# Cross-attention and gated feed-forward on one core: attention scores in quarters of the array, stacking transfers over all partitions

## The reference, cut to what matters

```python
q = (layernorm(x) @ Wq.T + bq); k = ctx @ Wk.T + bk; v = ctx @ Wv.T + bv     # split in 16 heads of 8
attn = softmax(q @ k.T / sqrt(8)) @ v;  x = x + attn @ Wo.T + bo
h = layernorm(x)
score_out, score_in = softmax(bottleneck_so(h)), softmax(bottleneck_si(h))   # batch norm over all rows, gelu
out  = keep_top32(score_out) * (h @ W) + (h * keep_top32(score_in)) @ W + bias
x = x + out
```

## Time and profile before

| | us |
|---|---|
| median of 3 runs | 564.16 |
| lowest, highest | 558.95, 564.75 |
| the profiled execution | 563.33 |
| its span | 560.8 |

### The profile page before, as it was taken

One profiled execution on the slowest core, in us unless ns is written; L12 is line 12 of the kernel. 1 busy time (PEld: TensorE's weight loads), 2 busy tenths in 40 slices (PEclk: granted clock), 3 DMA queues, 4 the chain that ended last, 5 costly groups with the idle time before them and its releaser, 6 DMA issues.

```text
span 560.8 us, 15570 instructions
## 1 busy us (share of the span) xinstructions
PE 405.9 (72%) x5186; PEld 316.1 (56%) x5186; DVE 440.5 (79%) x2165; ACT 375.1 (67%) x1060; POOL 330.2 (59%) x402
## 2 busy tenths in 40 slices
PE   3467988999998999988992766666666666666432
PEld 1135766777777777777860545545555555445331
DVE  7745666777877777776541799999999999999990
ACT  2425676877788777766655967777677666676652
POOL 6466676887677777562112046666666666666666
PEclk9857999999999999999795555555555555555555
DMA  4888786888887887675000000000000000000000
GB/s 135 177 206 207 193 199 151 194 185 185 192 195 191 206 187 185 161 168 123 4 4 1 0 2 19 19 20 20 19 20 19 20 20 19 20 20 19 19 20 19
DMA packets 138680, 52.78 MB, mean 94 GB/s; under 512 B 105115, under 2 KB 130908, under 8 KB 137052
## 3 DMA queue, kind: packets, MB, share of 16 engines
q1 hardware_dynamic: 136424, 51.27, 37.8%
q10 hardware_dynamic: 2176, 0.52, 0.4%
HBM read 34.47 MB, written 16.78 MB: 91 GB/s over the span
## 4 chain that ended last, share of the span: by engine, by line
DVE 41%; SPq 33%; DMA 9%; PE 7%; issue 5%; POOL 2%; ACT 2%; POOLq 0%; ACTq 0%; DVEq 0%
SPq L273 30%; DVE kst L868 22%; DVE top_next L859 12%; DMA k_scratch<-k_parts 6%; DVE top_first L859 4%; DMA qst<-q_scratch 3%; SPq L258 3%; PE ps_pv L329 1%; PE ps_col L314 1%; POOL kst L963 1%; ACT x2n L550 1%; PE ps_mix L534 1%; PE ps_row L358 1%; PE ps_row L503 1%; SPq L220 1%
## 5 line engine op out<-in xcount | busy, mean ns | idle before, releaser
L738 DVE TENSOR_REDUCE m<-ps_row 128x8 f32<-128x512 f32 x128 | 82.4, 686 | 54.5 <-PE ps_row L358 54.2
L868 DVE MATCH_REPLACE8 kst<-top_next,kst 128x128 f32<-128x128 f32 x384 | 101.2, 282 | 0.0
L545 ACT ACTIVATE pT<-ps_col 128x512 f32<-128x512 f32 x128 | 68.7, 589 | 37.1 <-PE ps_col L314 37.1
L859 DVE MAX8 top_next<-kst 128x8 f32<-128x128 f32 x384 | 78.2, 282 | 0.0
L329 PE MATMUL ps_pv<-vx,pT 128*64 128x18 f32 x2048 | 72.5, 213 | 0.0
L329 PEld LDWEIGHTS ps_pv<-vx,pT 128*64 128x64 f32 x2048 | 66.1, 139 | 6.3 <-issue 4.2
L519 PE MATMUL ps_proj<-wf_sb,x2T 128*128 128x128 f32 x128 | 33.2, 441 | 45.8 <-ACT x2T L682 45.8
L519 PEld LDWEIGHTS ps_proj<-wf_sb,x2T 128*128 128x128 f32 x128 | 28.5, 328 | 52.2 <-ACT x2T L682 52.2
L550 ACT ACTIVATE x2n<-xr,nm,rs 128x128 f32<-128x128 f32 x128 | 52.6, 493 | 4.2 <-POOL nm L888 4.2
L959 POOL TENSOR_SCALAR neg_max<-top_first 128x4 f32<-128x4 f32 x32 | 7.1, 222 | 74.8 <-DVE top_first L859 74.8
L358 PE MATMUL ps_row<-kst,qst 96*64 96x128 bf16 x1024 | 42.3, 226 | 12.1 <-DMA qst<-q_scratch 12.0
(11 more groups left out here) (103 smaller groups left out, 1092.7 us busy)
## 6 DMA issues: line engine op xcount, KB each, us to landing
k_scratch<-k_parts SPq DMA_DIRECT2D x32, 192.0 KB, 3.1
q_scratch<-q_parts SPq DMA_DIRECT2D x32, 192.0 KB, 3.0
kst<-k_scratch SPq DMA_DIRECT2D x32, 192.0 KB
qst<-q_scratch SPq DMA_DIRECT2D x32, 192.0 KB
xr<-in_x_dram SPq DMA_DIRECT2D x16, 256.0 KB, 4.3
cT<-in_ctxT_dram SPq DMA_DIRECT2D x16, 256.0 KB, 3.7
kst<-k_scratch SPq DMA_DIRECT2D x32, 128.0 KB
qst<-q_scratch SPq DMA_DIRECT2D x32, 128.0 KB
```

What stands on the lines that cost most here:

```text
L545: act.activation(pT[:, b % PT_RING, :, :], ps_col[b % 2][:, :, :], ACT.Exp, scale=SCALE).then_inc(act_exp, 1)
L738: dve.tensor_reduce(m32[:, b // 4, :, 4 * j:4 * j + 4].rearrange("q a h -> q h a"), ps_row[b % 2][:, :, :, :], AX.X, ALU.max).then_inc(dve ...
L859: ins = dve.max(top[:, n, :], src)
L868: ins = dve.match_replace(picked[s][:, p, cols], top[:, n, :], src, PICKED)
```

## The change

- Scores: `qst` and `kst` become the two halves of one tensor `stacks`, `kst` with a row of 8 KB like `qst`. Batch `a` has rows 64a to 64a+63 of the contraction. Every row or column matmul is now 64 rows by 64 columns with 64 moving columns, one for each pair and batch, issued in turn over the four quarters of the array: 128 and 128 a group in place of 64 and 64.
- Stacking: three pairs of transfers, each with both batches and two parts, so that 32 rows four partitions apart go out in one DMA; one more DMA sets the four maxima rows of `qst` to zero first. 7 a group in place of 12. Both scratch writes must have landed before any of them. The wait for `act_mT` ahead of them goes; the maxima DMA (on ScalarE's queue in both kernels, as the diff shows) waits for `moved` instead.
- Order: in each quarter of an iteration TensorE does `key_side` and `query_side` back to back, VectorE's steps are ordered anew, `values` pairs its operands by batch, the queries' split on GpSimd waits for the first maxima.
- Start: weights are loaded on ScalarE's queue, VectorE splits the first keys, and part of the first and last layer norm's small steps go to VectorE.
- Where the stages meet: the gelu table is loaded before the last gates, most of the batch norm's constants are worked out on VectorE, and the two repeated norms move behind the first gelu.
- Tail: the last group's final sums go to VectorE, gate by gate and in halves.

```diff
-RUNS = (3, 2, 1)
-STRIDE = 4
-MROWS = 2 * ROWS
-KROWS = MROWS + 4
+MID, HIGH, LOW = 0, 1, 2
+RUNS = ((MID, MID), (HIGH, MID), (MID, HIGH))
+MAX_ROWS = slice(3, 128, 32)
-STACK = 16 * 2 * len(RUNS)
+STACK = 16 * (2 * len(RUNS) + 1)
...
-        qst = [sb(f"qst{s}", [128, HEADS, HALF], BF16) for s in range(STACKS)]
-        kst = [sb(f"kst{s}", [128, HEADS, PAIRS, 2, SEQ], BF16) for s in range(STACKS)]
+        stacks = [sb(f"stacks{s}", [128, 2, HEADS, HALF], BF16) for s in range(STACKS)]
+        qst = [stacks[s][:, 0, :, :] for s in range(STACKS)]
+        kst = [stacks[s][:, 1, :, :] for s in range(STACKS)]
...
+        scratch = [nc.dram_tensor(f"scratch{s}", (2, 2 * PARTS, 128, HALF), BF16).ap() for s in range(2)]
...
+            def two_parts(g, first):
+                return scratch[g % 2][:, first:first + 2].rearrange("a n (i h) t -> a (n i) (h t)", h=HEADS)
+            def stack(g):
+                s, d = g % 2, slot(g)
...
+                wait(sp, k_out[s], WRITES * (g // 2 + 1))
+                wait(sp, q_out[s], WRITES * (g // 2 + 1))
+                wait(sp, pe_col, 8 * (g - STACKS + 1))
+                sp.dma_start(qst[d][MAX_ROWS, :, :].rearrange("r h t -> r (h t)"), fixed_rows[4:8]).then_inc(moved[d], 16)
+                for run, (q_first, k_first) in enumerate(RUNS):
+                    rows = slice(run, 128, 4)
+                    sp.dma_start(kst[d][rows, :, :].rearrange("r h t -> r (h t)"),
+                                 two_parts(g, PARTS + k_first)).then_inc(moved[d], 16)
+                    sp.dma_start(qst[d][rows, :, :].rearrange("r h t -> r (h t)"),
+                                 two_parts(g, q_first)).then_inc(moved[d], 16)
...
                 if there(t + 1):
-                    wait(sp, act_mT, 2 * t)
-                    wait(sp, pe_col, 8 * (t - 1))
-                    stack(t + 1, k_scratch, k_out, k_moved, True)
-                    stack(t + 1, q_scratch, q_out, q_moved, False)
+                    stack(t + 1)
...
+                for hh in range(HEADS // 2):
+                    h = j * (HEADS // 2) + hh
+                    for pp, a in ((0, 0), (1, 1), (1, 0), (0, 1)):
+                        rows = slice(a * 64, a * 64 + 64)
+                        cols = slice((2 * hp + pp) * SEQ, (2 * hp + pp + 1) * SEQ)
+                        mm = pe.matmul(ps_row[a][pp * SEQ:(pp + 1) * SEQ, hh, :], qst[s][rows, h, cols], kst[s][rows, h, cols],
+                                       start=True, stop=True)
...
-                wait(act, pe_col, 8 * (g - STACKS + 1))
+                wait(act, moved[slot(g)], STACK * uses(g))
                 wait(act, act_mT, 2 * g + hp + 1)
-                act.dma_start(qst[slot(g)][MROWS:KROWS, :, hp * 128:(hp + 1) * 128],
-                              mT[:, hp, :]).then_inc(m_moved[hp][slot(g)], 16)
+                act.dma_start(qst[slot(g)][MAX_ROWS, :, hp * 128:(hp + 1) * 128], mT[:, hp, :]).then_inc(m_moved[hp][slot(g)], 16)
...
-            again(0)
-            again(1)
-            act.wait_ge(dve_half, 2)
             act.activation(nothing[:, 1:2], nothing[:, 0:1], ACT.Gelu)
```

More of the change, by code:

```diff
@@ L236, in _, with write_parts @@
             sp.dma_start(gates[2 * GATES:2 * GATES + 1, :], ones_row).then_inc(rest_in, 16)
[L237 to L247, removed]
+            def write_parts(g, parts, first, done):
                 s = g % 2
                 if parts is k_parts:
-                    wait(sp, gp_split, 4 * g + 4)
+                    wait(sp, dve_ksplit, 4)
+                    wait(sp, gp_split, 4 * g)
                 else:
@@ L262, in stack @@
+            def stack(g):
                 s, d = g % 2, slot(g)
[L263 to L273, removed]
+                if g < STACKS:
+                    wait(sp, gp_zero if g == 1 else dve_zero, 1 + g // 2)
+                    sp.dma_start(kst[d][MAX_ROWS, :, :].rearrange("r h t -> r (h t)"), fixed_rows[0:4]).then_inc(rows_in[d], 16)
+                wait(sp, k_out[s], WRITES * (g // 2 + 1))
[8 more added lines that the diff above has]
+                                 two_parts(g, q_first)).then_inc(moved[d], 16)
@@ L305, in key_side @@
                     wait(pe, m_moved[hp][s], 16 * uses(g))
[L306 to L316, removed]
+                wait(pe, act_exp, 8 * g + 4 * hp + 2 * j)
+                for hh in range(HEADS // 2):
[3 more added lines that the diff above has]
+                        cols = slice((2 * hp + pp) * SEQ, (2 * hp + pp + 1) * SEQ)
+                        mm = pe.matmul(ps_col[a][pp * SEQ:(pp + 1) * SEQ, hh, :], kst[s][rows, h, cols], qst[s][rows, h, cols],
+                                       start=True, stop=True)
+                        if hh == HEADS // 2 - 1 and pp != a:
+                            mm.then_inc(pe_col, 1)
             def values(g, hp, j):
@@ L346, in out_proj, with query_side @@
                 mm.then_inc(pe_out, 1)
[L348 to L360, removed]
+            def query_side(g, hp, j):
+                s = slot(g)
+                if hp == 0 and j == 0:
+                    wait(pe, moved[s], STACK * uses(g))
+                    if g < STACKS:
+                        pe.wait_ge(rows_in[s], 16)
+                wait(pe, dve_max, 8 * g + 4 * hp + 2 * j)
+                for hh in range(HEADS // 2):
+                    h = j * (HEADS // 2) + hh
+                    for pp, a in ((0, 0), (1, 1), (1, 0), (0, 1)):
+                        rows = slice(a * 64, a * 64 + 64)
+                        cols = slice((2 * hp + pp) * SEQ, (2 * hp + pp + 1) * SEQ)
+                        mm = pe.matmul(ps_row[a][pp * SEQ:(pp + 1) * SEQ, hh, :], qst[s][rows, h, cols], kst[s][rows, h, cols],
+                                       start=True, stop=True)
+                        if hh == HEADS // 2 - 1 and pp != a:
+                            mm.then_inc(pe_row, 1)
             def turn_max(g, hp):
@@ L431, in _ @@
                     key_side(t - 1, 0, 0)
+                if c:
+                    query_side(t, 0, 0)
                 if e:
@@ L644, in _ @@
                     wait(act, gp_rs2, 4 * (t - 2) + 4)
+                    wait(act, dve_nm2, 1 if t - 2 == GROUPS - 1 else 0)
                     wait(act, pe_x2T, t - 3)
@@ L696, in _ @@
                             ins.then_inc(a2_exp, 1)
-                if there(t - 1):
+                if there(t - 1) and t < GROUPS:
                     s = (t - 1) % 2
@@ L854, in _ @@
                         else:
-                            wait(dve, d2_rep, 8 * g + 2 * rnd - 1 + half)
-                        for n in range(4 * half, 4 * half + 4):
+                            wait(dve, d2_rep, 8 * g + 2 * rnd - 1 + (1 if by_gate else half))
+                        for n in sets[half]:
                             p, cols = chain(n)
```

372 lines of the change are left out of this document (223 added, 149 removed).

## The result

| | before, us | after, us |
|---|---|---|
| median (4 runs each) | 563.23 | 883.25 |
| lowest, highest | 558.95, 564.75 | 882.87, 884.4 |
| span of the profiled execution | 560.8 | 881.1 |
| mean granted TensorE clock | 0.737 | 0.643 |

The changed kernel takes 1.574 times as long, 95% interval 1.566 to 1.581. The forecast was 917 us, within 855 to 1,020.

What follows compares the result with a forecast made beforehand. Stage 1 was taken to run at the pace of transfers and their issues, TensorE close behind. First stacking 22.2, fifteen periods 567, last transfers 32.8, to first MAX8 49, to end 244: span 915, plus 2.5, 917 us; range 855 to 1,020.

Steps and rivals of the forecast that it cites:

- The count of engines: Stacking transfers in stage 1: batch outermost in the source, 2 blocks of 16 rows, so each transfer uses 2 DMA engines.
- all six transfers fall to the same two: Stacking in stage 1: assumed that a group's six transfers share two engines, 96 rows of 8 KB on each.
- The price of a group: Stage 1 period: rows 30.5, zero row 0.3, writes 2.8, maxima 0.6, round trip 3.6, together 37.8 us; ends 34.5 and 42.7.
- round trip: Between groups in stage 1: scratch writes queue behind stacking, the next stacking waits for their landing; 3.6 us nothing covers.
- The row price of 0.318 us: Stacking on two engines: 318 ns per 8 KB row, from a line through output transfers and scratch writes; 30.5 us for 96.
- the first stacking: Start of the kernel: left at 22.2 us to the first stacking, 4 either way.
- the joint: Where the stages meet, last row scores to first MAX8: 45.9 us, less 2, plus 5 for the lower clock: 49.
- The wait that was put at nothing: Maxima transfer in stage 1: its added wait for `moved` is met already, since the row scores feeding it waited likewise.
- The lower clock: TensorE in half-idle stage 1: up to 36 us a group, still under 37.8, so it adds nothing there.
- Tail and joint: Second stage: tail saves 6 us (3 to 8), leaving 244 from first MAX8; the stretch before it takes 49.
- Rival 1: Stage 1 transfers find many engines; TensorE's 13.2 us a group sets the pace: 523 us, chance 0.10.
- Rival 2: Stage 1 transfers find many engines, but every quarter matmul takes 29 ns; TensorE 18.1 us a group: 597 us, chance 0.05.

Runs made afterwards that it cites:

- the cut in two: Changed kernel with each stacking transfer split in two by batch, 12 transfers of 16 rows in place of 6: 559.47 us, ratio 0.997 to the kernel before.
- the kernel with the keys first: Changed kernel with all stacking transfers split by batch, and the six key transfers issued before the wait for the queries' write: 545.8 us, ratio 0.975 to the kernel before.

## Why the prediction was right

**The count of engines was right, and it carried the forecast.** The step "its source has the batch `a` outermost ... by the count above that is 2 engines" is shown by the packets (two a transfer), by the DMA share of 0.12 and by the cut in two that takes 324 us away. The assumption that all six transfers fall to the same two is borne out by the same 0.12, taken while all six were outstanding. The Trainium skill ("DMA: Bandwidth & Descriptors", section "Why a DMA increments its semaphore by 16 and not by 1") has transfers run on the lowest-numbered engines; the share and the held-up maxima transfer agree with that, though no view here names the engines.

**The price of a group was 2 us high.** Forecast 37.8, measured 35.8. From the first row issue (307.09) to the row scores that the last row releases (340.10) it is 33.0 us, where rows, zero row and maxima made 31.4. From there to the next first row issue (342.74) it is 2.6, where writes and round trip made 6.4. The forecast added the writes and the round trip, and the trace has them in part at the same time: the last write was issued before the last row landed, and its landing follows that row by some 2 us. The row price of 0.318 us held (0.32 to 0.33 in the quiet stretches). Times fifteen the 2 us is 30 of the 34 us that the span came out lower. The rest is the first stacking (1.9 us) and the joint (2.8). What the forecast did not have is that the writes' issues stand in SyncE's queue for 24 us a group; they stand there while the rows move, so the period shows nothing of it.

**The wait that was put at nothing.** "The added wait of the maxima transfer for `moved` is met already" is true of the wait, and missed the transfer behind it: TensorE waits up to 7.4 us at a time for its landing. The total shows nothing of it, since the rows set the period and the chain by line does not name this transfer.

**The lower clock** was granted as forecast (0.67 in 100 to 200 us) and did not decide: TensorE is busy 44.8 of these 100 us, and waits for the rows in every group.

**Tail and joint** came as summed: 5.2 us off the second stage (249.9 to 244.7) for a forecast 6, and 46.2 us from row scores to first MAX8 for a forecast 49: of the 5 us put there for the lower clock some 2.3 came, if the 2 for the table load came in full. One end of the forecast has a slip: with the 3.6 us round trip hidden, 37.8 leaves 34.2 and not 34.5 us, which moves the low end by some 5 us and decides nothing.

**The rivals, had they come.** Rival 1 (523 us) was too quick. It put TensorE at 12.5 us a group and 13.2 with its joints; the kernel with the keys first, where TensorE is the bound, shows 13.6 busy and 14.54 with its joints, and 545.8 us. It also took the wait for both writes as free. That holds behind the two engines; with sixteen, the landing of the queries' write stands open on SyncE's queue, and with thirteen stacking issues it makes TensorE wait for SyncE. Whether seven issues on sixteen engines would hide it is open: no source layout that gives them was tried. Rival 2 is wrong in its mechanism, since a quarter matmul costs 8.6 ns and not 29 beside the three others.

So the 883 us are the two engines. What the rest of the change gives with sixteen, the profile of the kernel with the keys first shows against that of the kernel before: 4.1 us in stage 2 (249.9 to 245.8), 3.1 at the start (22.20 to 19.07), and in stage 1 the 0.8 us a group by which 14.54 stands below 15.34. From the last group's stacking to the first MAX8 it loses 3.4 us (58.5 to 62.0). Which part of the change brings which of these was not taken apart.

## What to carry to other kernels

A transfer that joins two others must be looked at from both sides: its DRAM side had a batch of two outermost, and that count, not the 32 rows or the 256 KB, set how many engines moved it. The completion packets of a queue (its packets less the pieces that the shapes give) are a total that every rule on the number of engines has to meet, and they can be counted before anything is built. The length of an issue is not fixed: it grew from 1.37 to 10.70 us for the same two writes, and a wait put ahead of issues is in part taken out of them. Ahead of a DMA that waits for two landings, ask which of its data needs only one, and issue that first.

## What the runs showed of the hardware

- Issues of a write that has pieces for all sixteen engines took 10.70 and 13.42 us for two each, in place of 1.37 and 1.02, while two engines were laden. The other fourteen engines had their bursts around the ends of these issues.
- A small transfer on another engine's queue is not apart from it: TensorE waited up to 7.4 us for the 16 KB of maxima on ScalarE's queue while 8 KB rows of SyncE's were under way.
- Two DMA engines alone moved 49 to 51 GB/s in rows of 8 KB, 25 each.
- Matmuls of 64 rows by 64 columns and 64 moving columns start 8.6 ns apart in the mean when neighbours use different quarters, and 21.0 ns when eight in turn use one. Within one quarter it is 32 ns in both orders.
- With one wait more ahead of them, the same transfers took SyncE 13.6 us of issues a group in place of 14.7.
